# Expert rows added to the output in memory by indirect accumulating writes, in place of stored partial rows and a closing sum

## The chip, the cores and the metric

The kernel runs on one core of a Trainium2 chip. The metric is the device time of one execution in microseconds, as the median of several runs. The engines are called PE (TensorE), DVE (VectorE), ACT (ScalarE), POOL (GpSimd) and SP (SyncE); each runs its own queue of instructions in order and waits on semaphores.

## The reference

A small image tower over 64 images of 2 x 104 x 104: shifted patch tokens, a gated linear attention block, and a mixture of experts with the two best of 8 experts for each token. There are 64 x 170 = 10,880 tokens of 128 numbers. What bears on this case is the last block:

```python
xf = x.reshape(-1, D)                       # layer norm of h, 10880 x 128
logits = xf @ router_w
gate_vals, idx = jax.lax.top_k(logits, 2)
gates = jax.nn.softmax(gate_vals, axis=-1)
out = zeros_like(xf)
for e in range(8):
    h = relu(xf @ w1[e] + b1[e]) @ w2[e] + b2[e]
    y = layernorm(xf + h, gamma[e], beta[e])
    w = sum(where(idx == e, gates, 0.0), axis=-1)
    out = out + w[:, None] * y
result = h + out
```

So each output row is its row of h plus two gated expert rows.

## The kernel before

**Stages.** First the images are made into tokens (to about 240 us), then pairs of images go through attention and routing (32 pairs, to about 690 us), then the experts work on tiles of tokens, then a closing stage sums.

**Pair stage.** For each pair DVE, ACT and PE finish h and the routing. POOL scatters each token's normalised row, with its gate and its id in columns 128 and 129, twice into `x_slots`, a table in memory that is sorted by expert (L552, six scatters a pair). SP stores the pair's rows of h in memory (L408, L410).

**Tile stage.** There are `NTILE` = 92 tiles of 256 slots, every one for one expert. They are the worst case: tiles past the last real one hold padding rows. A helper `tiles` runs the engines' work with lags: in iteration i, SP has loaded tile i into one of six buffers `x_sl` (L429, after `y_ready` of tile i-6), PE transposes tile i and runs the first layer of tile i-1 and the second of i-2, ACT applies relu, DVE adds, normalises, scales and gates (tiles i-1 to i-5). POOL adds a bias to the input of tile i-1 (`with_bias`, L573, read by DVE in iteration i+2) and scatters the finished rows of tile i-5 (`scatter_y`, L579), in this order on its queue. A tile's 256 rows go out in two indirect DMAs of 128 rows of 512 bytes. A token's two experts have ids of their own (2 x token and 2 x token + 1), so all rows of `y_tokens` (21,760) are written once and no scatter has to wait for another. Padding ids lie out of bounds and their rows are dropped. DVE writes a tile's rows into one of two buffers `y_sl` and first waits until the scatters of the tile before last have landed:

```python
need(dve, y_gone[n % 2], 32 * (XBUF // 2 * u + n // 2))
```

**Closing stage.** In the tile stage, after the first six tile loads, SP has loaded all rows of h back from memory, spread as 85 rows to a partition (L435, 5.4 MB). When all scatters have landed, SP loads `y_tokens` in 17 parts of 5 rows and two experts for each partition (L449), DVE adds both to h (L1339, 34 adds), and ACT's queue stores the 17 parts in `out` (L1561).

Of the kernel before, what the change touches and what calls it, by code (L numbers as in the profile page):

```python
# [37 lines left out]
FC = FF // 128  # L38
YBUF = 8
PART_ROWS = NTOK // 128  # L40
SUM_ROWS = 5
NSUM = PART_ROWS // SUM_ROWS
XBUF = 6
# [4 lines left out]
XW = 130  # L48
PAD_ID = 2 * NTOK
LAST_TILE_LAG = 5  # L50
# [20 lines left out]
def const_array():  # L71
    cols, width = const_layout()
    c = np.zeros((128, width), np.float32)

    def put(name):
        a, b = cols[name]
        return c[:, a:b]

    put("ident")[:] = np.eye(128)

    wt = np.array([1 if m in (0, HGRID - 1) else 2 for m in range(HGRID)] * GROUP, np.float32)
    img_h = np.repeat(np.arange(GROUP), HGRID)
    img_m = np.concatenate([np.repeat(np.arange(GROUP), GRID), np.full(HROWS - MROWS, -1)])
    for k, img in enumerate((img_h, img_m)):
        same = (img_h[:, None] == img[None, :]).astype(np.float32)
        put("stat_all")[:HROWS, k * HROWS:(k + 1) * HROWS] = same * (1 + 2 * wt[:, None])
        put("stat_edge")[:HROWS, k * HROWS:(k + 1) * HROWS] = -same * wt[:, None]
    s = np.arange(CHUNK)
    put("causal")[:CHUNK] = s[:, None] <= s[None, :]
    r = np.arange(128)  # L90
    put("before")[:] = r[:, None] < r[None, :]
    put("eo")[:] = (r[:, None] // HK) % 2 == np.arange(2)[None, :]
    h = np.arange(128) // HV
    put("meanv")[:] = (h[:, None] == h[None, :]) / HV
    put("reset")[:] = (np.arange(TOK) % CHUNK != 0)[None, :]
    put("cls_sel")[0, :PT] = np.arange(PT) % TOK != 0
    put("cls_sel")[1, :PT] = np.arange(PT) % TOK == 0
    put("expert")[:] = np.arange(8)
    put("region")[:] = np.arange(8) * REGION
    put("eps")[:, 0:5] = [EPS_TOK, EPS_LN, EPS_GN, EPS_FFN, 1.0]  # L100
    put("eps")[:, 5] = -1 / 16
    put("eps")[:, 6] = 1 / 16
    put("tokid")[:] = 2 * (r[:, None] + 128 * np.arange(PTILES)[None, :])
    put("slotid")[:] = np.arange(128)[:, None] + 128 * np.arange(2)[None, :]
    put("tiles_k")[:] = SLOT * np.arange(43)
    put("one_row")[:] = 1
    return c


def need(eng, sem, value):  # L110

    if not isinstance(value, int) or value > 0:
        eng.wait_ge(sem, value)
# [44 lines left out]
def build(nc, a, out_rows):  # L158

    cols, cwidth = const_layout()  # L160
    xs_dram = nc.dram_tensor("x_slots", (NEXP * REGION + SLOT, XW), F32, kind="Internal").ap()
    h1_dram = nc.dram_tensor("h1_rows", (NTOK, E_DIM), F32, kind="Internal").ap()
    y_dram = nc.dram_tensor("y_tokens", (2 * NTOK, E_DIM), F32, kind="Internal").ap()

    with ExitStack() as ctx:
# [75 lines left out]
        def two(*shape, **kw):  # L241
# [55 lines left out]
        y_id = [A3.take(2, dt=I32) for _ in range(2)]  # L297
        y_tok = [A3.take(SUM_ROWS, 2, E_DIM) for _ in range(YBUF)]
        h1_rows = h[:, :, :, :].rearrange("p a c n -> p (a c n)")[:, 0:PART_ROWS * E_DIM]
        assert A3.at <= PHASE1_WORDS  # L300
# [8 lines left out]
            "c_loaded z_prep w_loaded small_loaded prep_done xl0 xl1 edge_done dsum_done asum_done "  # L309
            "stat_ps var_done h_out h1_stored h1_loaded ln1_stats ln1_rstd xn_ready xnt_ps xnt_sb qk_ps carry_ps g_ps v_ps "  # L310
            "l_ready scan_done e_ready g_copied g_ready v_ready qk_ready sc_ps att_ready kt_ps kt_ready "
# [5 lines left out]
            "xs1 xs2 xs3 xs4 xs5 norm_ready scl_ready gate_ready bns3_ready xt_ps xhi_ready xlo_ready "  # L317
            "h_ps h_ready w2_ps xb_ready t_ready rstd3_stats rstd3_ready y_ready yg0 yg1 yl0 yl1 yl2 yl3 "
            "yl4 yl5 yl6 yl7 sum_ready rstd0_done nb_done xmn_done xhn_done tr_full tr_free y_full "
            "h_added dch ach pch t_prep d_prep xen_done "  # L320
# [9 lines left out]
        TOKEN_BANKS = (4, 5, 7, 4)  # L330
        y_loaded = [S[f"yl{n}"] for n in range(YBUF)]
        LAST_LAG = 5
# [57 lines left out]
        def expert_sync(sp):  # L390
# [14 lines left out]
            with sp.Fori(0, PAIRS) as p:  # L405
                sp.wait_ge(S["h1_ready"], p + 1)
                full = 128 * (PTILES - 1)
                sp.dma_start(h1_dram[bass.ds(p * PT, full), :].rearrange("(c r) n -> r c n", r=128),  # L408
                             h[:, bass.ds(p, 1), 0:PTILES - 1, :].rearrange("p o c n -> p (o c) n")).then_inc(S["h1_stored"], 16)
                sp.dma_start(h1_dram[bass.ds(p * PT + full, PREST), :],  # L410
                             h[0:PREST, bass.ds(p, 1), PTILES - 1, :].rearrange("p o n -> p (o n)")).then_inc(S["h1_stored"], 16)
# [20 lines left out]
            for n in range(XBUF):  # L432
                load(n, n)
            sp.wait_ge(S["h1_stored"], 32 * PAIRS)
            sp.dma_start(h1_rows, h1_dram.rearrange("(p j) n -> p (j n)", p=128)).then_inc(S["h1_loaded"], 16)  # L435
            with sp.Fori(1, NTILE // XBUF) as u:
                for n in range(XBUF):
                    load(XBUF * u + n, n)
            for i in range(NTILE // XBUF * XBUF, NTILE):
                load(i, i % XBUF)  # L440


            for gone in y_gone:
                sp.wait_ge(gone, 32 * (NTILE // 2))

            y_part = y_dram.rearrange("(p j k) n -> p j k n", p=128, k=2)
            for c in range(NSUM):
                need(sp, S["sum_ready"], 2 * (c - YBUF + 1))
                sp.dma_start(y_tok[c % YBUF], y_part[:, SUM_ROWS * c:SUM_ROWS * c + SUM_ROWS]).then_inc(y_loaded[c % YBUF], 16)  # L449

# [61 lines left out]
        def _(pool):  # L512
# [44 lines left out]
            pool.memset(pad_row[:, :, 0:129], 0.0).then_inc(S["pad_ready"], 1)  # L557
            pool.memset(pad_row[:, :, 129:130], float(PAD_ID)).then_inc(S["pad_ready"], 1)

# [15 lines left out]
            def scatter_y(i, n, u, e):  # L575
                pool.wait_ge(S["y_ready"], i + 1)
                apart(pool)
                for k in range(2):
                    pool.indirect_dma_start(  # L579
                        y_dram, bass.IndirectOffsetOnAxis(ap=y_id[n % 2][:, k:k + 1], axis=0),  # L580
                        y_sl[n % 2][:, k, :], None, bounds_check=2 * NTOK - 1, oob_is_err=False,
                    ).then_inc(y_gone[n % 2], 16)

# [3 lines left out]

            pool.wait_ge(S["tab_ready"], 1)
            tiles(pool, Chain(pool, None), 0, 0, tile_iteration)


# [307 lines left out]
        def _(dve):  # L899
# [277 lines left out]
            def gates(p, par):  # L1177
# [4 lines left out]
                ch.step(dve.reciprocal(row[p % ROWS][:, 0, :, 128], den[:, :]))  # L1182
                dve.tensor_scalar(row[p % ROWS][:, 1, :, 129], ids[:, :], 1.0, None, ALU.add).then_inc(S["gate_done"], 1)

            def place(p, par):
# [3 lines left out]
                ch.step(dve.tensor_tensor(row[p % ROWS][:, 1, :, 128], row[p % ROWS][:, 0, :, 128], edif[:, :], ALU.mult))  # L1189
                ch.link(dve.tensor_scalar(ids[:, :], ids[:, :], float(2 * PT), None, ALU.add))  # L1190
                dve.tensor_copy(slot_i[p % ROWS][:], slot_f[:]).then_inc(S["slots_ready"], 1)  # L1191
# [25 lines left out]
            ch.link(dve.memset(om[:, PTILES:PTILES + 1], 0.0))  # L1217
            ch.link(dve.memset(o_f[:, PT:PCOLS], 0.0))
            dve.tensor_copy(ids[:, :], con("tokid")).then_inc(S["base_ready"], 1)  # L1219
            dve.wait_ge(S["base_ready"], 1)  # L1220
# [85 lines left out]
            def shifted(i, n, u, e):  # L1306
# [3 lines left out]

                need(dve, y_gone[n % 2], 32 * (XBUF // 2 * u + n // 2))
                ch.step(dve.tensor_copy(y_id[n % 2], x_sl[n][:, :, E_DIM + 1]))
# [18 lines left out]
            dbase = tiles(dve, ch, dbase, DVE_TILE, tile_iteration)  # L1331


            dve.wait_ge(S["h1_loaded"], 16)
            for c in range(NSUM):
                dve.wait_ge(y_loaded[c % YBUF], 16 * (c // YBUF) + 16)
                rows = h1_rows[:, SUM_ROWS * E_DIM * c:SUM_ROWS * E_DIM * (c + 1)].rearrange("p (j n) -> p j n", n=E_DIM)
                for k in range(2):
                    dve.tensor_tensor(rows, rows, y_tok[c % YBUF][:, :, k, :], ALU.add).then_inc(S["sum_ready"], 1)  # L1339
                    dve.wait_ge(S["sum_ready"], 2 * c + k + 1)  # L1340


        @block.scalar
        def _(act):
# [211 lines left out]

            out_part = out_rows.rearrange("(p j) n -> p (j n)", p=128)
            for c in range(NSUM):
                act.wait_ge(S["sum_ready"], 2 * c + 2)
                part = slice(SUM_ROWS * E_DIM * c, SUM_ROWS * E_DIM * (c + 1))  # L1560
                act.dma_start(out_part[:, part], h1_rows[:, part]).then_inc(S["h_out"], 16)  # L1561
            act.wait_ge(S["h_out"], 16 * NSUM)

# [26 lines left out]
```

## Time and profile before

| what | value |
|---|---|
| median of 3 runs | 1102.32 us (1100.51 to 1102.33) |
| profiled execution, its own time | 1104.65 us |
| span in its profile | 1102.9 us |
| mean granted clock of PE | 0.853 |
| first scatter of tile 0, last scatter of tile 91 (start) | 721.0 us, 1057.1 us |
| last part summed | from 1098.6 us |

Times in the profile count from the start of the span. A row of the timeline gives the start, the duration, engine, line, operation and, in brackets, the idle time of the engine before it with what ended it. "issue" there means that nothing which the profile shows was waited for. The duration of a DMA_INDIRECT on POOL is the time that POOL works on it; its rows land later. In a DMA row each digit is the busy share, in tenths, of the 16 DMA engines in one of 40 equal slices of the window (9 is 90% or more).

### The profile page before, as it was taken

To read this page: it belongs to the slowest core of one execution; us is meant where nothing else is said; L and a number is where in the kernel's file an instruction comes from. 1 tells how busy PE (TensorE), PEld (TensorE's weight loads), DVE (VectorE), ACT (ScalarE), POOL (GpSimd) and SP (SyncE) were. 2 spreads that over 40 slices of the span, in tenths; PEclk is the share of its full clock that TensorE was granted. 3 is DMA by queue.
4 is the path that set the end of the run, shared out by engine and by line. 5 is a ranking of instruction groups with operands and counts; after the bars stand their busy time and mean duration, and the time that the engine had idled before them with its cause. 6 is when DMAs were issued, how large, how long until landed. Compare 5 with 4: busy or idle time off the path is not lost.

```text
span 1102.9 us, 27762 instructions
## 1 busy us (share of the span) xinstructions
PE 880.8 (80%) x7792; PEld 730.5 (66%) x7793; DVE 789.5 (72%) x3172; ACT 554.0 (50%) x1512; POOL 445.1 (40%) x491
## 2 busy tenths in 40 slices
PE   1577888879899999988989973499999999899900
PEld 1467888865676666666667652388888888888800
DVE  1488887754766666667776655189999998899956
ACT  0212111006867666677787642266666666566600
POOL 3000000000144444444554445267777777777720
PEclk9989888898867777789997765699999999999955
DMA  7363441015011111111111111632222222222259
GB/s 132 62 94 51 67 65 23 1 57 165 24 37 43 40 40 40 39 42 50 45 46 47 42 45 40 204 137 75 67 71 70 72 69 66 70 70 73 61 210 397
DMA packets 69073, 84.09 MB, mean 76 GB/s; under 512 B 12051, under 2 KB 53702, under 8 KB 68858
## 3 DMA queue, kind: packets, MB, share of 16 engines
q1 hardware_dynamic: 54282, 54.93, 20.2%
q0 software_dynamic: 12256, 22.50, 6.6%
q10 hardware_dynamic: 2448, 5.57, 1.3%
q8 instruction: 46, 0.75, 0.3%
q14 instruction: 41, 0.34, 0.1%
HBM read 48.15 MB, written 35.71 MB: 76 GB/s over the span
## 4 chain that ended last, share of the span: by engine, by line
PE 52%; issue 14%; DVE 13%; ACT 8%; DMA 5%; another core or an unknown queue 3%; SPq 2%; DVEq 1%; POOL 1%; ACTq 0%; POOLq 0%
PE ps L650 7%; PE ps L885 6%; DVE arena L986 4%; PE ps L706 4%; PE ps L876 4%; PE ps L874 3%; PE ps L731 3%; DMA arena<-y_tokens 3%; PE ps L717 3%; PE ps L875 3%; PE ps L799 2%; PE ps L712 2%; PE ps L766 2%; PE ps L785 2%
## 5 line engine op out<-in xcount | busy, mean ns | idle before, releaser
L552 POOL DMA_INDIRECT x_slots<-arena x192 | 184.2, 959 | 264.2 <-DVE arena L1191 66.5
L579 POOL DMA_INDIRECT y_tokens<-arena x184 | 184.7, 1004 | 46.2 <-issue 43.8
L1538 ACT ACTIVATE arena<-ps,b_t 128x256 f32<-128x256 f32 x368 | 156.8, 478 | 88.3 <-PE ps L876 80.2
L885 PE MATMUL ps<-arena 128*128 x1472 | 181.0, 276 | 0.0
L885 PEld LDWEIGHTS ps<-arena 128*128 128x128 f32 x1472 | 171.6, 192 | 1.9
L650 PE MATMUL ps<-wt,arena 128*128 128x128 f32 x960 | 131.0, 299 | 8.7 <-DVE h L1008 8.7
L650 PEld LDWEIGHTS ps<-wt,arena 128*128 128x128 f32 x960 | 125.6, 213 | 10.2 <-DVE arena L986 10.2
L874 PE MATMUL ps<-arena 128*128 128x256 f16 x368 | 101.5, 276 | 21.2 <-DVE arena L1263 12.4
L1401 ACT ACTIVATE arena<-ps 128x340 f32<-128x340 f32 (+3 forms) x160 | 70.0, 447 | 65.8 <-PE ps L793 24.2
L876 PE MATMUL ps<-arena 128*128 128x256 f16 x368 | 100.9, 274 | 0.0
L875 PE MATMUL ps<-arena 128*128 128x256 f16 x368 | 100.9, 274 | 0.0
L573 POOL TENSOR_TENSOR arena<-arena 128x256 f32<-128x256 f32 x92 | 66.4, 721 | 66.1 <-issue 34.7
L1294 DVE TENSOR_SCALAR arena<-arena 128x128 f32<-128x128 f32 x184 | 88.8, 531 | 3.4
L986 DVE TENSOR_TENSOR arena<-ps,arena 128x312 f32<-128x312 f32 (+2 forms) x160 | 71.1, 502 | 27.2 <-PE ps L636 27.2
L557 POOL MEMSET arena<- 128x258 f32 x1 | 0.3, 318 | 201.4 <-DVE arena L1219 201.4
L1263 DVE TENSOR_TENSOR arena<-ps,arena 128x256 f16<-128x256 f32 x92 | 38.8, 422 | 43.3 <-ACT arena L1530 40.7
L1102 DVE TENSOR_TENSOR arena<-ps,cst 85x340 f32<-85x340 f32 x128 | 59.6, 501 | 13.0 <-PE ps L731 7.7
L874 PEld LDWEIGHTS ps<-arena 128*128 x368 | 35.8, 97 | 39.9 <-issue 34.0
L731 PE MATMUL ps<-arena 32*85 32x170 f32 x512 | 59.2, 353 | 1.6 <-DVE arena L1093 1.6
L1315 DVE SCALAR_TENSOR_TENSOR arena<-arena 128x128 f32<-128x128 f32 x184 | 56.6, 349 | 0.0
L636 PE MATMUL ps<-cst,arena 112*128 112x112 f32 (+1 forms) x216 | 33.2, 286 | 26.6 <-DVE arena L969 26.6
L799 PEld LDWEIGHTS ps<-rw,arena 128*128 128x128 f32 x192 | 35.0, 260 | 28.5 <-ACT arena L1401 16.2
(203 smaller groups left out, 1844.4 us busy)
## 6 DMA issues: line engine op xcount, KB each, us to landing
arena<-x_slots SPq DMA_DIRECT2D x92, 130.0 KB
arena<-y_tokens SPq DMA_DIRECT2D x17, 640.0 KB, 14.8
h<-h_rows SPq DMA_DIRECT2D x1, 5440.0 KB
out<-h ACTq DMA_DIRECT2D x17, 320.0 KB, 9.5
arena<-x_in SPq DMA_DIRECT2D x64, 84.5 KB
arena<-x_in SPq DMA_DIRECT2D x64, 78.0 KB
h_rows<-h SPq DMA_DIRECT2D x32, 128.0 KB
x_slots<-arena POOLq DMA_INDIRECT x192
```

Of the source, the lines that this page charges most:

```text
L552: pool.indirect_dma_start(xs_dram, bass.IndirectOffsetOnAxis(ap=slot_i[n][0:rows, t, k:k + 1], axis=0), row[n][0:rows, k, t, :], None).the ...
L579: pool.indirect_dma_start(y_dram, bass.IndirectOffsetOnAxis(ap=y_id[n % 2][:, k:k + 1], axis=0), y_sl[n % 2][:, k, :], None, bounds_check= ...
L650: ins = pe.matmul(ps[TOKEN_BANKS[pair]][:, 128 * t:128 * t + 128], gx_all[par][:, s, at:at + 128], wt[:, s, :], start=s == 0, stop=s == NS ...
L731: ins = pe.matmul(o, kd[par][r, chunk(c)], qd[par][r, :, chunk(c)], start=True, stop=True, tile_position=(at, 0))
L874: pe.matmul(o, hi, x_hi[m], start=True, stop=False)
L875: pe.matmul(o, hi, x_lo[m], start=False, stop=False)
L876: pe.matmul(o, lo, x_hi[m], start=False, stop=True).then_inc(S["h_ps"], 1)
L885: ins = pe.matmul(ps[6 + m][:, 128 * k:128 * k + 128], hid[m][:, c, 128 * k:128 * k + 128], w2_sb[:, bass.ds(e, 1), c, :].rearrange("p o n ...
L986: return dve.tensor_tensor(dst, src, gm, ALU.mult)
L1294: ins = dve.tensor_scalar(nrm[:, k, :], res[n % 2][:, k, :], mv3[:, k, 0:1], rg3[:, k:k + 1], ALU.subtract, ALU.mult)
L1401: act.activation(dst, src, ACT.Copy).then_inc(S[done], 1)
L1538: act.activation(hid[m][:, c, :], ps[2 + 2 * m + c // 2][:, SLOT * (c % 2):SLOT * (c % 2) + SLOT], ACT.Relu, bias=b1_t[:, bass.ds(e * FC + ...
```

## The change

The rows of h are stored straight into `out`, which has 256 rows more than there are tokens. Both expert rows of a token carry the token's own id, and the scatters add to `out` in memory instead of writing to `y_tokens`. The two experts of a token are in different tiles, so POOL waits, before it scatters a tile, until both scatters of the tile ahead have landed. Padding rows are given ids in the 256 extra rows, which are cleared by two small stores from POOL; no bounds check is left, and padding rows are written too. The load of h, the 17 loads of partial rows, the 34 sums and the 17 stores are dropped, and POOL waits at its end for the last scatters.

```diff
-YBUF = 8
+YBUF = 2
-PAD_ID = 2 * NTOK
+OUT_ROWS = NTOK + SLOT
-    put("tokid")[:] = 2 * (r[:, None] + 128 * np.arange(PTILES)[None, :])
+    put("tokid")[:] = r[:, None] + 128 * np.arange(PTILES)[None, :]
...
-                sp.dma_start(h1_dram[bass.ds(p * PT, full), :].rearrange("(c r) n -> r c n", r=128),
+                sp.dma_start(out_rows[bass.ds(p * PT, full), :].rearrange("(c r) n -> r c n", r=128),
...
-            sp.wait_ge(S["h1_stored"], 32 * PAIRS)
-            sp.dma_start(h1_rows, h1_dram.rearrange("(p j) n -> p (j n)", p=128)).then_inc(S["h1_loaded"], 16)
...
-            for gone in y_gone:
-                sp.wait_ge(gone, 32 * (NTILE // 2))
-            y_part = y_dram.rearrange("(p j k) n -> p j k n", p=128, k=2)
-            for c in range(NSUM):
-                need(sp, S["sum_ready"], 2 * (c - YBUF + 1))
-                sp.dma_start(y_tok[c % YBUF], y_part[:, SUM_ROWS * c:SUM_ROWS * c + SUM_ROWS]).then_inc(y_loaded[c % YBUF], 16)
...
-            pool.memset(pad_row[:, :, 129:130], float(PAD_ID)).then_inc(S["pad_ready"], 1)
+            pool.wait_ge(S["pad_ready"], 2)
+            for m in range(YBUF):
+                pool.dma_start(out_rows[NTOK + 128 * m:NTOK + 128 * m + 128, :], pad_row[:, m, 0:E_DIM]).then_inc(y_gone[m], 16)
...
             def scatter_y(i, n, u, e):
                 pool.wait_ge(S["y_ready"], i + 1)
+                pool.wait_ge(y_gone[(n - 1) % YBUF], 16 + 32 * (XBUF // YBUF * u + (n - 1) // YBUF + 1))
                 apart(pool)
                 for k in range(2):
                     pool.indirect_dma_start(
-                        y_dram, bass.IndirectOffsetOnAxis(ap=y_id[n % 2][:, k:k + 1], axis=0),
-                        y_sl[n % 2][:, k, :], None, bounds_check=2 * NTOK - 1, oob_is_err=False,
-                    ).then_inc(y_gone[n % 2], 16)
+                        out_rows, bass.IndirectOffsetOnAxis(ap=y_id[n % 2][:, k:k + 1], axis=0),
+                        y_sl[n % 2][:, k, :], None, compute_op=ALU.add,
+                    ).then_inc(y_gone[n % YBUF], 16)
...
             pool.wait_ge(S["tab_ready"], 1)
+            pool.wait_ge(S["h1_stored"], 32 * PAIRS)
+            for gone in y_gone:
+                pool.wait_ge(gone, 16)
             tiles(pool, Chain(pool, None), 0, 0, tile_iteration)
+            for gone in y_gone:
+                pool.wait_ge(gone, 16 + 32 * (NTILE // YBUF))
...
-                dve.tensor_scalar(row[p % ROWS][:, 1, :, 129], ids[:, :], 1.0, None, ALU.add).then_inc(S["gate_done"], 1)
+                dve.tensor_copy(row[p % ROWS][:, 1, :, 129], ids[:, :]).then_inc(S["gate_done"], 1)
...
-                need(dve, y_gone[n % 2], 32 * (XBUF // 2 * u + n // 2))
+                dve.wait_ge(y_gone[n % YBUF], 16 + 32 * (XBUF // YBUF * u + n // YBUF))
...
-            dve.wait_ge(S["h1_loaded"], 16)
-            for c in range(NSUM):
-                dve.wait_ge(y_loaded[c % YBUF], 16 * (c // YBUF) + 16)
-                rows = h1_rows[:, SUM_ROWS * E_DIM * c:SUM_ROWS * E_DIM * (c + 1)].rearrange("p (j n) -> p j n", n=E_DIM)
-                for k in range(2):
-                    dve.tensor_tensor(rows, rows, y_tok[c % YBUF][:, :, k, :], ALU.add).then_inc(S["sum_ready"], 1)
-                    dve.wait_ge(S["sum_ready"], 2 * c + k + 1)
...
-            out_part = out_rows.rearrange("(p j) n -> p (j n)", p=128)
-            for c in range(NSUM):
-                act.wait_ge(S["sum_ready"], 2 * c + 2)
-                part = slice(SUM_ROWS * E_DIM * c, SUM_ROWS * E_DIM * (c + 1))
-                act.dma_start(out_part[:, part], h1_rows[:, part]).then_inc(S["h_out"], 16)
-            act.wait_ge(S["h_out"], 16 * NSUM)
```

## Rows read from the trace of the kernel before

**Rows 1.** The page: its span and its 40 slices, tenths of each.

```profile
span 1102.9 us, 27762 instructions
...
PEclk9989888898867777789997765699999999999955
...
DMA  7363441015011111111111111632222222222259
```

**Rows 2.** Windows of 100 us over tiles: engines' busy us and counts, clock, DMA share, GB/s.

```profile
740.00:840.00 100.00, 94.44 (x814) 85.65 (x812) 91.85 (x355) 63.64 (x190) 73.79 (x82) 1.00 0.26 71
...
sum 300.00, PE 281.24 PEld 256.05 DVE 272.94 ACT 191.39 POOL 221.04; mean PE 93.75 PEld 85.35 DVE 90.98 ACT 63.80 POOL 73.68
```

**Rows 3.** Timeline, POOL alone, one tile.

```profile
802.69 0.71 POOL L573 TENSOR_TENSOR arena<-arena 128x256 f32<-128x256 f32 x1 [0.51 <-issue]
...
803.56 1.00 POOL L579 DMA_INDIRECT y_tokens<-arena  x1 [0.15 <-issue]
...
804.86 0.98 POOL L579 DMA_INDIRECT y_tokens<-arena  x1 [0.30 <-issue]
...
806.33 0.72 POOL L573 TENSOR_TENSOR arena<-arena 128x256 f32<-128x256 f32 x1 [0.49 <-issue]
```

**Rows 4.** One line's instructions, L579: ns min/median/max, first and last start.

```profile
L579 POOL DMA_INDIRECT y_tokens<-arena x184: 982/998/1225, 721.0 to 1057.1; - x184
```

**Rows 5.** Timeline, the first tiles.

```profile
701.06 6.13 SPq L429 DMA_DIRECT2D arena<-x_slots  x6
...
703.30 0.29 PEld L859 LDWEIGHTS ps<-cst,arena 128*128 128x128 f32 x2 [14.23 <-DMA arena<-x_slots]
...
707.23 0.47 SPq L435 DMA_DIRECT2D h<-h_rows  x1
...
721.00 1.03 POOL L579 DMA_INDIRECT y_tokens<-arena  x1 [0.16 <-issue]
...
724.59 0.73 POOL L573 TENSOR_TENSOR arena<-arena 128x256 f32<-128x256 f32 x1 [1.15 <-issue]
```

**Rows 6.** Timeline, last scatters and the closing stage.

```profile
1055.86 0.98 POOL L579 DMA_INDIRECT y_tokens<-arena  x1 [0.31 <-issue]
1057.14 0.98 POOL L579 DMA_INDIRECT y_tokens<-arena  x1 [0.30 <-issue]
1059.32 22.52 SPq L449 DMA_DIRECT2D arena<-y_tokens  x17
1063.21 6.83 DVE L1339 TENSOR_TENSOR h<-h,arena 128x640 f32<-128x640 f32 x8 [8.28 <-DMA arena<-y_tokens]
...
1098.58 1.68 DVE L1339 TENSOR_TENSOR h<-h,arena 128x640 f32<-128x640 f32 x2 [0.66 <-DMA arena<-y_tokens]
```

**Rows 7.** Groups by line, closing stage: busy us, mean ns | idle before, releaser.

```profile
L1339 DVE TENSOR_TENSOR h<-h,arena 128x640 f32<-128x640 f32 x34 | 28.0, 825 | 17.3 <-DMA arena<-y_tokens 16.6
```

**Rows 8.** DMA view, 805.84 to 807.20 us, behind a tile's second scatter.

```profile
DMA  0000000000000000399973000000000000000000
...
DMA packets 32, 0.07 MB, mean 48 GB/s; under 512 B 16, under 2 KB 16, under 8 KB 32
```

**Rows 9.** DMA view, 1057.0 to 1059.3 us, last scatters.

```profile
DMA  0000000011000000000000000000001100000000
...
DMA packets 64, 0.00 MB, mean 1 GB/s; under 512 B 64, under 2 KB 64, under 8 KB 64
```

**Rows 10.** DMA view, 701.0 to 703.4 us, the first tile load.

```profile
DMA  0000000000000000003965999886321000000445
```

**Rows 11.** One line's instructions, L552.

```profile
L552 POOL DMA_INDIRECT x_slots<-arena x192: 920/957/1211, 294.0 to 694.0; - x192
```

**Rows 12.** Windows of the pair stage and of the first tiles, columns as in rows 2.

```profile
448.00:452.00 4.00, 2.71 (x22) 1.89 (x21) 2.42 (x15) 2.17 (x7) 1.34 (x2) 1.00 0.12 33
452.00:456.00 4.00, 4.00 (x20) 2.51 (x19) 2.45 (x8) 3.56 (x12) 1.90 (x2) 0.50 0.07 21
...
700.00:710.00 10.00, 4.63 (x24) 3.11 (x25) 0.85 (x2) 2.34 (x6) 1.36 (x2) 0.60 0.54 150
```

More of the change, by code:

```diff
@@ L38 @@
 FC = FF // 128
-YBUF = 8
-PART_ROWS = NTOK // 128
-SUM_ROWS = 5
-NSUM = PART_ROWS // SUM_ROWS
+YBUF = 2
 XBUF = 6
@@ L161, in build @@
     xs_dram = nc.dram_tensor("x_slots", (NEXP * REGION + SLOT, XW), F32, kind="Internal").ap()
-    h1_dram = nc.dram_tensor("h1_rows", (NTOK, E_DIM), F32, kind="Internal").ap()
-    y_dram = nc.dram_tensor("y_tokens", (2 * NTOK, E_DIM), F32, kind="Internal").ap()
     with ExitStack() as ctx:
@@ L297, in build @@
         y_id = [A3.take(2, dt=I32) for _ in range(2)]
-        y_tok = [A3.take(SUM_ROWS, 2, E_DIM) for _ in range(YBUF)]
-        h1_rows = h[:, :, :, :].rearrange("p a c n -> p (a c n)")[:, 0:PART_ROWS * E_DIM]
         assert A3.at <= PHASE1_WORDS
@@ L309, in build @@
             "c_loaded z_prep w_loaded small_loaded prep_done xl0 xl1 edge_done dsum_done asum_done "
-            "stat_ps var_done h_out h1_stored h1_loaded ln1_stats ln1_rstd xn_ready xnt_ps xnt_sb qk_ps carry_ps g_ps v_ps "
+            "stat_ps var_done h1_stored ln1_stats ln1_rstd xn_ready xnt_ps xnt_sb qk_ps carry_ps g_ps v_ps "
             "l_ready scan_done e_ready g_copied g_ready v_ready qk_ready sc_ps att_ready kt_ps kt_ready "
@@ L317, in build @@
             "xs1 xs2 xs3 xs4 xs5 norm_ready scl_ready gate_ready bns3_ready xt_ps xhi_ready xlo_ready "
-            "h_ps h_ready w2_ps xb_ready t_ready rstd3_stats rstd3_ready y_ready yg0 yg1 yl0 yl1 yl2 yl3 "
-            "yl4 yl5 yl6 yl7 sum_ready rstd0_done nb_done xmn_done xhn_done tr_full tr_free y_full "
+            "h_ps h_ready w2_ps xb_ready t_ready rstd3_stats rstd3_ready y_ready yg0 yg1 "
+            "rstd0_done nb_done xmn_done xhn_done tr_full tr_free y_full "
             "h_added dch ach pch t_prep d_prep xen_done "
@@ L330, in build @@
         TOKEN_BANKS = (4, 5, 7, 4)
-        y_loaded = [S[f"yl{n}"] for n in range(YBUF)]
         LAST_LAG = 5
@@ L407, in expert_sync @@
                 full = 128 * (PTILES - 1)
-                sp.dma_start(h1_dram[bass.ds(p * PT, full), :].rearrange("(c r) n -> r c n", r=128),
+                sp.dma_start(out_rows[bass.ds(p * PT, full), :].rearrange("(c r) n -> r c n", r=128),
                              h[:, bass.ds(p, 1), 0:PTILES - 1, :].rearrange("p o c n -> p (o c) n")).then_inc(S["h1_stored"], 16)
-                sp.dma_start(h1_dram[bass.ds(p * PT + full, PREST), :],
+                sp.dma_start(out_rows[bass.ds(p * PT + full, PREST), :],
                              h[0:PREST, bass.ds(p, 1), PTILES - 1, :].rearrange("p o n -> p (o n)")).then_inc(S["h1_stored"], 16)
@@ L1189, in place @@
                 ch.step(dve.tensor_tensor(row[p % ROWS][:, 1, :, 128], row[p % ROWS][:, 0, :, 128], edif[:, :], ALU.mult))
-                ch.link(dve.tensor_scalar(ids[:, :], ids[:, :], float(2 * PT), None, ALU.add))
+                ch.link(dve.tensor_scalar(ids[:, :], ids[:, :], float(PT), None, ALU.add))
                 dve.tensor_copy(slot_i[p % ROWS][:], slot_f[:]).then_inc(S["slots_ready"], 1)
@@ L1218, in _ @@
             ch.link(dve.memset(o_f[:, PT:PCOLS], 0.0))
+            dve.tensor_scalar(pad_row[:, :, 129], con("slotid"), float(NTOK), None, ALU.add).then_inc(S["pad_ready"], 1)
             dve.tensor_copy(ids[:, :], con("tokid")).then_inc(S["base_ready"], 1)
@@ L1587 @@
         aps[name] = nc.dram_tensor(name + "_in", arr.shape, DT.from_np(arr.dtype), kind="ExternalInput").ap()
-    out = nc.dram_tensor("out", (NTOK, E_DIM), F32, kind="ExternalOutput").ap()
+    out = nc.dram_tensor("out", (OUT_ROWS, E_DIM), F32, kind="ExternalOutput").ap()
     build(nc, aps, out)
     r = run_bass_kernel_spmd(nc, [arrays], core_ids=[0])
-    return r.results[0]["out"].reshape(BATCH, TOK, E_DIM)
+    return r.results[0]["out"][:NTOK].reshape(BATCH, TOK, E_DIM)
```

## The prediction

> **What bounds the kernel now.** I read the page first: the last two slices show the DMA engines at five and nine tenths after a long stretch at two, and PE's clock, granted in full through that stretch, at half [rows 1]. Two stages matter, the expert tiles and the closing stage.
>
> The three windows of 100 us over the tile stage show PE busy 94%, DVE 91% and POOL 74% on the mean, with the DMA engines at a quarter [rows 2]. That makes POOL look the least loaded of the three. The timeline of POOL says otherwise [rows 3]: a bias add of 0.72 us, 0.15 us, the first scatter (1.00), 0.30, the second scatter (0.98), and 0.49 until the next bias add: 3.64 us from one bias add to the next. The gaps are put down to "issue", that is to no other engine, and the 0.30 between two scatters stays when nothing else is left to do [rows 6]. So POOL is walked through without a real wait: its queue is as full as PE's. First scatter of tile 0 at 721.00 and first scatter of tile 91 at 1055.86 [rows 4, 6] give the mean period: 334.86 / 91 = 3.68 us.
>
> The closing stage lies bare. The last scatter ends at 1057.14 + 0.98 = 1058.12; SP loads the partial rows from 1059.32, DVE's first sum starts at 1063.21, the last pair of sums at 1098.58, and the span ends at 1102.9 [rows 6]. The sums take 34 x 0.824 = 28.0 us and wait 16.6 us for their loads [rows 7]. From the last scatter's end to the end of the span: 44.8 us.
>
> **What goes.** All of those 44.8 us, except what the last scatter needs to land. The single load of the stored rows into h (SP, 707.23 [rows 5]) goes too. It moves 5.4 MB while tiles 0 to 5 are already in SBUF or on their way; the first reload behind it feeds tile 6, and POOL then shows a gap of 1.15 us [rows 5]. Tile 0's first scatter at 721.00 comes after DVE's first result and not after this load. I cost the removal at nothing if POOL paces the tiles, since an early slip is then absorbed, and at 1 to 2 us gained if it doesn't. The two pad stores that POOL now issues early stand ahead of its first slot scatter at 294.0 [rows 11], whose data the pair stage has yet to make, so they are covered; without that cover they cost two issues of about 1 us. The ids count tokens instead of twice tokens and one add of 1 becomes a copy: one small DVE operation for another, nothing. The wait for the stored rows ahead of the tile loop is nothing too: they stand on SP's queue ahead of the slot loads, and PE waits 14.23 us for the first of those [rows 5].
>
> **What comes in.** Scatter of tile i may not start before both scatters of tile i-1 have landed. Behind that wait on POOL stand its own two scatters and the bias add of tile i+5; that add is used by DVE two tiles later, so DVE follows only when POOL is slower on the whole. DVE's own wait, for the rows of tile i-2, is then always met ahead of time, or one period behind POOL.
>
> The loop on POOL becomes: end of the second scatter, R until the next tile's first scatter may start, first scatter, gap, second scatter. P = R + 1.00 + 0.30 + 1.00 = R + 2.30.
>
> R for plain rows can be read. In the closing case nothing else moves: generation ends at 1058.12 and SP, which waits for this landing, issues at 1059.32: 1.20 us [rows 6]. That scatter moved no rows (0.00 MB in the window), and its small packets pass in slices 31 and 32 of a window of 2.3 us, so until 0.72 us after its end [rows 9]. For a scatter with rows I take the second scatter of a full tile: its generation ends at 805.84 [rows 3], and from there the rows pass in slices 17 to 22 of a window of 1.36 us, that is from 0.54 to 0.75 us after the end, and the small packets behind them [rows 8]. That is about 0.1 us later than the empty one: R = 1.3 us. Today POOL's bias add and its gaps take 0.49 + 0.72 + 0.15 = 1.36 us in the same place [rows 3]. A plain landing would thus be hidden to the last tenth, and P = 3.6, under the 3.68 of today.
>
> But the rows are now added, so each of 128 rows of 512 bytes must be read from HBM before it is written. No row shows this. Lower bound of the extra: 0, if the read is hidden under the descriptor work. Upper bound: a whole further transfer, as the first slot load: issued at 701.06, PE released by it at 703.30, so 2.2 us [rows 5]. Its packets begin only in slice 19 of 40 (2.4 us from 701.00, so at about 702.1) [rows 10]: about 1.0 us of it is the issue, of which the scatter has its own within R, and 1.2 us are the trip with its burst. I take 0.9 us, nearest to that trip, and less than it because the scatter's burst is shorter (0.2 us against some 0.8). R = 1.3 + 0.9 = 2.2 and P = 4.5 us.
>
> Generation: 1.00 us for a scatter with a bounds check, 0.957 us for the one without [rows 4, 11]. The check goes (-0.04), the add may need more descriptor work (unknown; bound above by a half more, 1.5 us, if a row needs a second source beside its source and destination; below by 0.96). I take 1.00.
>
> **Sum.** T = 721.00 + 91 P + 2.30 + R + 0.3 (end of program) = 721.00 + 409.5 + 2.3 + 2.2 + 0.3 = 1135.3 us of span. Against the profiled execution's own span of 1102.9 that is +32.4: the 44.8 us of the closing stage less 2.5 for the last landing are won, 42.3; the tiles cost 91 x (4.50 - 3.68) = 74.6. The profiled execution took 1104.65, the median is 1102.32; moved by the same difference the forecast is 1135 us. The change pays only while 92 R < 1102.9 - 723.6 - 209.3 = 170.0, so R < 1.85 us: half a microsecond beyond a plain landing is what it can bear. Everything hangs on that.
>
> Two rules of the Trainium skill speak against my 0.9. "DMA: Bandwidth & Descriptors", section "Latency and other measured facts", gives 0.2 us for an average HBM access and 2 us at high load. No row here shows an access by itself. As an estimate from that page, with 0.2 us the period would be 3.8 and the span about 1071 us, with 2 us 5.6 and about 1236 us. The same page, section "Two DMAs through the same engine are not ordered", reports that a second read-modify-write of a row read stale data when it directly followed the first and no longer with five packets between. No run here shows this either. By it the write trails the read by some packets only, and a packet run as short as [rows 8] would make the extra a fraction of a microsecond, which is rival A.
>
> **Rivals.**
> A, faster: the read of the old row is hidden. The eight rows of each DMA engine pass in one burst of 0.2 us (16 large packets for 0.07 MB beside 16 small ones, so 4 KB each) [rows 8]; if read and write overlap as closely, R stays between 1.3 and 1.85. At 1.3 the tiles keep 3.68 and T = 721.0 + 334.9 + 2.3 + 1.3 + 0.3 = 1059.8, -43 us, so 1059. It decides from R = 1.85 down. For it speaks the short burst and DMA engines three quarters idle; against it that every row needs two memory trips in order.
> B, generation grows to 1.5 us: P = 2.2 + 3.3 = 5.5, T = 1227. Nothing in the profile prices it.
> C, the read is a full transfer of 2.2 us: R = 3.5, P = 5.8, T = 1255. Beyond it, the eight rows of an engine go one after the other, 8 x 0.9: P = 10.8 and over 1700 us.
> D, PE's clock: with P = 4.5 PE is busy 3.45 us of a tile (93.75% of 3.68 [rows 2]), 77%. The pair stage shows PE busy 2.71 of 4 us at full clock and the next 4 us at half [rows 12]. If the clock is at half for half the time, a tile needs 3.45 / 0.75 = 4.6 us, just above 4.5: T = 1144. Against it, the clock came back in the first 10 us of tiles with PE busy 4.63 of 10 us, and then stayed [rows 1, 12].
>
> **Chances.** Likeliest (extra 0.6 to 1.4 us) 0.50, with its own range 1107 to 1181. A 0.22, of which 0.02 lands within 0.2% of before (2.2 us, about what a measurement of this kernel can tell from no change). B 0.12, C 0.08, its serial form 0.04, D 0.04. Faster 0.20, same 0.02, slower 0.78. The range of 1070 to 1235 leaves out the best part of A (some 0.08) and C with its serial form (0.12).
>
> **What would show it.** In the changed trace POOL's first scatter of a tile should be released by a DMA onto out, not by "issue", and start R after the end of the second scatter: 2.2 us right, below 1.85 and the forecast's sign is wrong. The scatters' own duration tells B. The windows should show PE at about 77% and POOL about 60% at a granted clock of 1.00; lower tells D. Nothing should follow the last scatter but its landing. A second burst or a longer one behind each scatter would show where the read sits.

## The result and the profile after

| what | before | after |
|---|---|---|
| median | 1102.32 us | 1296.92 us (1293.95 to 1305.03, 4 runs) |
| ratio | 1 | 1.178, 95% interval 1.172 to 1.185 |
| profiled execution, its own time and span | 1104.65, 1102.9 us | 1293.95, 1292.1 us |

The sign was right, the size was not: 17.8% slower where 3% was forecast, and 62 us above the upper end of the range. Ratios and ranges, here and below, leave out executions at a lower granted clock that took over 1.5% longer than the fastest of the same kernel, such as one of the kernel before at 1122.55 us.

The page of the changed kernel, its span, clock and DMA slices, POOL's busy slices and its costliest group; beside [rows 1, 4]:

```profile
span 1292.1 us, 27549 instructions
...
POOL 2000000003444444444443466666666666666664
PEclk9988888895886779789655997988898989898985
DMA  7353320411111111111113233323332333333322
...
L563 POOL DMA_INDIRECT out<-arena x184 | 298.7, 1623 | 204.3 <-issue 113.0
...
L556 POOL TENSOR_TENSOR arena<-arena 128x256 f32<-128x256 f32 x92 | 113.9, 1238 | 24.6 <-DVE arena L1260 12.6
```

The scatters are L563 now and the bias adds L556. A scatter takes 1.62 us of POOL on the mean, against 1.00 in [rows 4]. The closing burst of the DMA engines is gone, and the tile stage runs to the end of the span.

POOL alone in the timeline, one tile in the middle and the last two tiles; beside [rows 3, 6]:

```profile
902.31 1.56 POOL L563 DMA_INDIRECT out<-arena  x1 [1.80 <-DMA out<-arena]
904.18 1.56 POOL L563 DMA_INDIRECT out<-arena  x1 [0.30 <-issue]
905.19 1.26 POOL L556 TENSOR_TENSOR arena<-arena 128x256 f32<-128x256 f32 x1
909.01 1.56 POOL L563 DMA_INDIRECT out<-arena  x1 [2.56 <-issue]
...
1277.27 1.56 POOL L563 DMA_INDIRECT out<-arena  x1 [2.43 <-issue]
1279.14 1.56 POOL L563 DMA_INDIRECT out<-arena  x1 [0.30 <-issue]
1283.12 1.56 POOL L563 DMA_INDIRECT out<-arena  x1 [2.42 <-issue]
1284.99 1.56 POOL L563 DMA_INDIRECT out<-arena  x1 [0.30 <-issue]
```

Tile 0's first scatter starts at 721.39, that of tile 91 at 1283.12: P = 561.73 / 91 = 6.17 us, against 3.68 before and 4.50 forecast. Without generation (2 x 1.623) and the gap of 0.30 that leaves R = 2.63 us on the mean; the undisturbed end shows 2.42. The idle time in brackets counts from the bias add where one lies between, and half of it is put down to "issue": the name of the releaser alone would not have told of the wait.

The wait itself is an instruction of POOL's sequencer. The same line's instructions in a small window that holds only the wait ahead of the scatter at 1283.12, columns as in [rows 4]:

```profile
L122 POOLq EVENT_SEMAPHORE  x1: 4852/4852/4852, 1277.5 to 1277.5; - x1
```

It is released at 1277.5 + 4.85 = 1282.4. The scatter ahead of it ended generating at 1280.70, so its rows landed 1.7 us later, and the next scatter starts 0.75 us after the release. R, the time from the end of a tile's second scatter to the start of the next tile's first, is thus made of two parts, 1.7 and 0.75.

The windows over tiles, columns as in [rows 2]:

```profile
740.00:840.00 100.00, 65.27 (x485) 57.30 (x485) 49.51 (x208) 38.71 (x113) 63.57 (x48) 0.90 0.31 43
...
sum 500.00, PE 327.47 PEld 288.20 DVE 248.74 ACT 195.82 POOL 321.35; mean PE 65.49 PEld 57.64 DVE 49.75 ACT 39.16 POOL 64.27
```

PE, DVE and ACT all stand at 39 to 65%: they follow POOL, which is itself busy only 64% and waits in its loop for the rest. DVE's wait ahead of its cast of the ids shows it, in the waits of 740 to 1240 us (engine and line, releaser: us in total, times, longest):

```profile
DVE arena L1302 <- DMA out<-arena: 242.1, 82, 4.6
...
POOL out L563 <- DMA out<-arena: 91.3, 49, 2.1
```

The DMA view behind the second scatter of the tile before the last, 1280.7 to 1283.1 us, beside [rows 8]:

```profile
DMA  0000000009995399999930000000000000000000
...
DMA packets 144, 0.07 MB, mean 27 GB/s; under 512 B 16, under 2 KB 144, under 8 KB 144
```

144 packets where a plain scatter has 32: every added row is a packet of its own (128, and 16 small ones), and they pass in slices 10 to 21 of 0.06 us, so from 0.54 to 1.26 us after the end of generation, where the plain rows were through at 0.75.

The end of the program, by line, last instructions:

```profile
L160 POOLq DRAIN  x1: 3413/3413/3413, 1288.4 to 1288.4; - x1
```

POOL drains for 3.4 us behind its last landing. Before, its drain (8.0 us from 1056.1) lay under the closing stage.

### The profile page after: what moved, and what is told of

The parts are those of the page before. It is cut to its first block and busy times, and to the rows that moved or that the text cites. A ratio compares the mean times of both kernels' runs of the same rounds, so it can differ in the third digit from the quotient of the medians.

```text
span 1292.1 us, 27549 instructions
## 1 busy us (share of the span) xinstructions
PE 933.9 (72%) x7792; PEld 770.2 (60%) x7793; DVE 734.4 (57%) x3139; ACT 557.1 (43%) x1512; POOL 560.0 (43%) x492
## 5 line engine op out<-in xcount | busy, mean ns | idle before, releaser
L563 POOL DMA_INDIRECT out<-arena x184 | 298.7, 1623 | 204.3 <-issue 113.0
L863 PE MATMUL ps<-arena 128*128 128x256 f16 x368 | 113.8, 309 | 182.1 <-DVE arena L1253 182.1
L874 PE MATMUL ps<-arena 128*128 x1472 | 196.9, 291 | 0.0
L874 PEld LDWEIGHTS ps<-arena 128*128 128x128 f32 x1472 | 189.4, 208 | 2.0
L1302 DVE CAST arena<-arena 128x2 int32<-128x2 f32 x92 | 15.5, 169 | 266.3 <-DMA out<-arena 266.3
L863 PEld LDWEIGHTS ps<-arena 128*128 x368 | 39.5, 107 | 206.2 <-issue 197.9
L1526 ACT ACTIVATE arena<-arena,cst 128x2 f32<-128x2 f32 x92 | 27.2, 295 | 275.1 <-DVE arena L1274 269.3
L556 POOL TENSOR_TENSOR arena<-arena 128x256 f32<-128x256 f32 x92 | 113.9, 1238 | 24.6 <-DVE arena L1260 12.6
L865 PE MATMUL ps<-arena 128*128 128x256 f16 x368 | 114.8, 312 | 0.0
L864 PE MATMUL ps<-arena 128*128 128x256 f16 x368 | 114.4, 311 | 0.0
L1284 DVE TENSOR_SCALAR arena<-arena 128x128 f32<-128x128 f32 x184 | 64.0, 463 | 3.4
L706 PE MATMUL ps<-wproj,arena 128*85 128x128 f32 x256 | 46.0, 336 | 14.0 <-ACT arena L1382 14.0
```

The lines of the kernel that those rows point to most:

```text
L556: pool.tensor_tensor(x_b2[n % 2], x_sl[n][:, :, 0:E_DIM], b2, ALU.add).then_inc(S["xb_ready"], 1)
L563: pool.indirect_dma_start(out_rows, bass.IndirectOffsetOnAxis(ap=y_id[n % 2][:, k:k + 1], axis=0), y_sl[n % 2][:, k, :], None, compute_op= ...
L863: pe.matmul(o, hi, x_hi[m], start=True, stop=False)
L864: pe.matmul(o, hi, x_lo[m], start=False, stop=False)
L865: pe.matmul(o, lo, x_hi[m], start=False, stop=True).then_inc(S["h_ps"], 1)
L874: ins = pe.matmul(ps[6 + m][:, 128 * k:128 * k + 128], hid[m][:, c, 128 * k:128 * k + 128], w2_sb[:, bass.ds(e, 1), c, :].rearrange("p o n ...
```

## The experiments

The experiments ran on three chips, on which the kernel before takes different times: 997 us on the chip of the first four, 1094 to 1110 us on the next, and 1069 to 1081 us on that of the last three (half the width and the second and third with float16). So each is compared with the runs of before beside it. On the chip of the first four the stage ahead of the tiles is shorter: the first scatter starts at 640 to 643 us, not at 721. The kernel before wasn't profiled there. Its period is worked out from its time: 997.45 - 1.75 (time less span, as in the profiled execution) - 44.8 (closing stage) - 2.3 (the last tile's two scatters and gap) - 641 = 307.6, by 91, 3.38 us.

**Plain writes, wait kept** (the add is left out, a row of out holds the last expert row):

```diff
-                        y_sl[n % 2][:, k, :], None, compute_op=ALU.add,
+                        y_sl[n % 2][:, k, :], None,
```

> The changed kernel with plain scatters instead of adding ones (the add is left out, so a row of out holds the expert row that came last); every wait stays. Theory 1, the add makes all of the loss: generation back at 0.96 to 1.00 us, R (end of a tile's second scatter to the start of the next tile's first) 1.3 us, period 3.68 us, about 1064 us. Theory 2, the wait has a price of its own, because POOL's sequencer can prepare the next scatter only once it is released: generation 1.00, R 1.2 + 0.75 = 1.95 us, period 4.25 us, about 1115 us. Theory 3, only the wait matters and plain rows land as late as added ones: R 2.4 to 2.6, period 4.8, about 1160 us with generation at 1.00, or 1290 us if the generation of 1.56 us comes from waiting too.

Measured: 1051.08 us against 997.45, ratio 1.052 (1.045 to 1.059). The scatters, then POOL's last tiles, then the wait ahead of the scatter at 1041.42:

```profile
L563 POOL DMA_INDIRECT out<-arena x184: 955/962/1257, 642.5 to 1042.7; - x184
```

```profile
1038.40 0.96 POOL L563 DMA_INDIRECT out<-arena  x1 [0.30 <-issue]
1041.42 0.96 POOL L563 DMA_INDIRECT out<-arena  x1 [2.06 <-issue]
```

```profile
L122 POOLq EVENT_SEMAPHORE  x1: 3257/3257/3257, 1037.4 to 1037.4; - x1
```

Generation is back at 0.96 us. R is 2.06 us: released at 1037.4 + 3.26 = 1040.66, so 1.3 us of landing and 0.76 us from the release to the scatter. The period is (1041.42 - 642.5) / 91 = 4.38 us, where theory 2 said 4.25. That is theory 2: waiting for a plain landing costs R = 2.06 and not 1.3, and 2.1 on the mean of all tiles. The end is dearer than thought: the last scatter's generation ends at 1043.64 and the span at 1051.3, 5.9 us of it POOL's drain.

**The wait alone**, on the kernel before:

```diff
                 pool.wait_ge(S["y_ready"], i + 1)
+                need(pool, y_gone[(n - 1) % 2], 32 * (XBUF // 2 * u + (n - 1) // 2 + 1))
```

> The kernel before with the wait alone: scatter of tile i waits for the landed rows of tile i-1, plain writes to the stored partial rows, closing stage kept. Theory 1 (the add makes the loss): R 1.3 us, period 3.68, 1102 us, no change. Theory 2 (the wait has a price of about 0.75 us in POOL's sequencer): R 1.95, period 4.25, plus 91 x 0.57 = 52 us, 1154 us. Theory 3 (plain rows land as late): R 2.4, period 4.7, 1195 us.

Measured: 1097.95 us, ratio 1.098 (1.090 to 1.106), +100 us. A tile of POOL in its timeline:

```profile
901.40 0.98 POOL L580 DMA_INDIRECT y_tokens<-arena  x1 [0.30 <-issue]
902.38 0.71 POOL L573 TENSOR_TENSOR arena<-arena 128x256 f32<-128x256 f32 x1
904.48 1.00 POOL L580 DMA_INDIRECT y_tokens<-arena  x1 [1.38 <-issue]
```

R = 904.48 - 902.38 = 2.10 here. The period over all tiles is 4.48 us. Against the 3.38 us of before that is 91 x 1.10 = 100 us, but as 3.38 was worked out from the same total, this only says that the start and the closing stage are as assumed; this trace has them, with the first scatter at 643.4 and 44.9 us from the last scatter's end to the end of the span. The expectation had the period nearly right (4.25) and the price wrong, because it took 3.68 for the kernel before. The bias add starts with no gap behind the scatter here, so the gap of 0.49 us ahead of it in [rows 3] was not POOL's own.

The sequencer's own instructions show what lies between the release and the scatter. The wait of this tile, the two moves that belong to the next scatter (902.38 to 904.48 us), and the same two moves of the kernel before, for the scatter at 803.56 of [rows 3]:

```profile
L125 POOLq EVENT_SEMAPHORE  x1: 2977/2977/2977, 900.7 to 900.7; - x1
```

```profile
L580 POOLq MOVE  x2: 29/29/29, 903.7 to 904.3; - x2
```

```profile
L579 POOLq MOVE  x2: 29/29/29, 802.7 to 803.3; - x2
```

The rows have landed at 900.70 + 2.98 = 903.68, 1.3 us after the end of generation. Only then come the moves, and the scatter 0.8 us behind the release. In the kernel before the moves ran at 802.7 and 803.3, under the bias add (802.69 to 803.40), and the scatter followed it after 0.15 us.

**The add alone**, on the kernel before, without the wait. Each stored row is touched once (SP fills them with rows of h in the pair stage, and POOL waits for that fill ahead of the tiles, so the output holds h three times). Of the edit only the scatter is shown:

```diff
-                        y_sl[n % 2][:, k, :], None, bounds_check=2 * NTOK - 1, oob_is_err=False,
+                        y_sl[n % 2][:, k, :], None, bounds_check=2 * NTOK - 1, oob_is_err=False, compute_op=ALU.add,
```

> The kernel before with adding scatters and no wait between tiles: each row of the stored partial rows is still touched once (SP fills them with rows of h in the pair stage first, so the output holds h three times); closing stage kept. Theory 1 and 2 agree that generation grows to 1.56 us a scatter without any wait: POOL's loop is 0.49 + 0.72 + 0.15 + 1.56 + 0.30 + 1.56 = 4.8 us, 1102 + 91 x 1.1 = about 1203 us, or 4.25 us and 1153 us if the bias add overlaps the scatter's end, as it does by 0.55 us in the changed trace. Rival: the longer generation comes from the missing bounds check or from waiting; then 1.00 us and 1102 us here.

Measured: 1091.31 us, ratio 1.092 (1.085 to 1.099), +94 us. By line, then one tile of the timeline:

```profile
L584 POOL DMA_INDIRECT y_tokens<-arena x184: 1562/1567/1809, 640.1 to 1045.3; - x184
```

```profile
805.40 1.57 POOL L584 DMA_INDIRECT y_tokens<-arena  x1 [0.17 <-issue]
807.27 1.56 POOL L584 DMA_INDIRECT y_tokens<-arena  x1 [0.30 <-issue]
808.27 1.27 POOL L578 TENSOR_TENSOR arena<-arena 128x256 f32<-128x256 f32 x1
809.71 1.57 POOL L584 DMA_INDIRECT y_tokens<-arena  x1 [0.16 <-issue]
```

The longer generation belongs to the adding form: it is there with the bounds check and without any wait. POOL is full here, its bias add even starts 0.56 us before the scatter ahead ends, and the next scatter follows 0.88 us behind that end. The period is 4.43 us (4.25 expected for a bias add that overlaps), 1.05 more than the 3.38 worked out for before.

**Half the rows** in each adding scatter (64 of 128; the other half of the expert rows is left out):

```diff
-                        out_rows, bass.IndirectOffsetOnAxis(ap=y_id[n % 2][:, k:k + 1], axis=0),
-                        y_sl[n % 2][:, k, :], None, compute_op=ALU.add,
+                        out_rows, bass.IndirectOffsetOnAxis(ap=y_id[n % 2][0:64, k:k + 1], axis=0),
+                        y_sl[n % 2][0:64, k, :], None, compute_op=ALU.add,
```

> The changed kernel with 64 rows in each adding scatter instead of 128 (the other half of the expert rows is left out). If descriptor generation goes by the row: 0.8 us a scatter, landing a little earlier, period about 4.4 us, about 1135 us. If it is a fixed cost of the adding form: 1.5 us a scatter, only the burst of packets is shorter (by half of 0.7 us), period 5.7 to 5.8 us, about 1250 us.

Measured: one run, 1162.1 us on the chip where before takes 997.45.

```profile
L563 POOL DMA_INDIRECT out<-arena x184: 1417/1419/1628, 640.8 to 1151.4; - x184
```

Half the rows take 1.42 of 1.57 us: generation is nearly all fixed. The period is 5.59 us (5.7 to 5.8 expected) and R 2.43 us on the mean. The total was missed (1250 expected) mostly by the start, 80 us earlier on this chip.

**Both kernels again**, on another chip:

> The kernel before, unchanged, for its profile on the chip of these runs. On the chip of the first four experiments it took 997 us, and the first scatters there started at 640 to 643 us instead of 721. If the pair stage alone is shorter, the period is still 3.68 us. From 997.45 less 1.75, less the 44.8 us of the closing stage, less 641 and 2.3: 308.6 / 91 = 3.39 us, so PE and not POOL's queue paces the tiles of the kernel before, and POOL's own shortest loop lies below 3.4 us.

> The changed kernel, unchanged, beside the kernel before on the chip of these runs. If POOL alone paces its tiles, the period stays 6.15 to 6.2 us, though PE is faster here: 641 + 91 x 6.17 + 3.4 + 5.5 + 1.8 = about 1213 us against 997, so +215 us. If the loss were tied to PE's clock, it would stay +194 us or shrink in proportion, 1175 to 1191 us.

The kernel before took 1102.62 us with its first scatter at 719.3 and the period 3.69 us, so on this chip it is the kernel of [rows 1 to 7] again; the first four experiments' chip wasn't met a second time, and its period for before stays worked out, not seen (307.6 us by 91; the 308.6 above is a slip). The changed kernel took 1296.27 us, ratio 1.175 (1.159 to 1.191), with a period of 6.16 us. The question asked of it, whether its loss is the same where the kernel before is faster, stays open for the whole kernel.

**The wait ahead of the bias add**, plain writes (the add is left out; `landed` holds the wait that stood in `scatter_y`):

```diff
             def tile_iteration(at):
+                at(5, landed)
                 at(1, with_bias)
                 at(5, scatter_y)
```

> The first experiment (plain writes, wait kept, add left out) with the wait for the landed rows moved ahead of the bias add on POOL. There the scatter started 0.76 us after the release of the wait. If these 0.76 us are POOL's sequencer preparing the scatter, it does so while the bias add runs: R = 1.31 + 0.1 + 0.7 + 0.15 = 2.25 to 2.35 us, period 4.5 to 4.6. If they are a delay of the release itself, they stand ahead of the bias add too: R = 1.31 + 0.76 + 0.7 + 0.15 = 2.9 us, period 5.15 us.

Measured: one run, 1178.54 us, period 4.89 us, R 2.6 on the mean, between the two forecasts. The timeline says why:

```profile
900.11 0.96 POOL L562 DMA_INDIRECT out<-arena  x1 [0.30 <-issue]
902.87 0.78 POOL L556 TENSOR_TENSOR arena<-arena 128x256 f32<-128x256 f32 x1 [1.80 <-DMA out<-arena]
903.81 0.98 POOL L562 DMA_INDIRECT out<-arena  x1 [0.16 <-issue]
```

The scatter now follows 0.16 us behind the bias add, so its preparation did run under it. But the bias add has a preparation too. The wait's instruction on POOL's sequencer ends at 902.39, 1.3 us behind 901.07, and the bias add starts 0.5 us after it, not 0.1; in between the sequencer works through its registers and one more wait. What stands first behind a wait pays for its own sequencer work, 0.5 us for this bias add, 0.76 for a scatter.

**Half the width** (adding scatters of 64 numbers a row; the other half of each row is left out and the rows land elsewhere in out):

```diff
-                        out_rows, bass.IndirectOffsetOnAxis(ap=y_id[n % 2][:, k:k + 1], axis=0),
-                        y_sl[n % 2][:, k, :], None, compute_op=ALU.add,
+                        out_rows.rearrange("r (a b) -> (r a) b", a=2), bass.IndirectOffsetOnAxis(ap=y_id[n % 2][:, k:k + 1], axis=0),
+                        y_sl[n % 2][:, k, 0:64], None, compute_op=ALU.add,
```

> The changed kernel with adding scatters of 64 numbers (256 bytes) a row instead of 128 numbers, 128 rows each; the other half of each expert row is left out and the rows land elsewhere in out. If the longer generation (1.57 us) is a cost of the adding form and not of bytes, it stays 1.5 to 1.6 us here. If the later landing comes from the bytes that each row reads and writes, the landing is 0.2 to 0.4 us earlier and R 2.2 to 2.4; if it comes from the trip of each row to memory and back, R stays 2.6. Period 5.8 to 6.2 us either way; by rival, a generation that goes by bytes, 0.8 us and period 4.6.

Measured: one run, 1262.4 us.

```profile
L563 POOL DMA_INDIRECT out<-arena x184: 1562/1565/1775, 705.1 to 1253.5; - x184
```

Generation doesn't know the width. The period is 6.01 us, 0.16 less than with the full width, of which R takes it all (2.46 on the mean against 2.63). In the drained end R is 2.43 ahead of the last tile, against 2.42. So half the bytes take off at most a third of the 0.5 us by which added rows land later on the mean, and nothing where no other work is left; whether the rest is the read of the old row or the passing of single packets, no run separates.

**A smaller closing stage instead.** If the closing stage can't be traded for adds, it can be made shorter: the kernel before with its partial rows in float16.

```diff
-    y_dram = nc.dram_tensor("y_tokens", (2 * NTOK, E_DIM), F32, kind="Internal").ap()
+    y_dram = nc.dram_tensor("y_tokens", (2 * NTOK, E_DIM), F16, kind="Internal").ap()
...
-        y_sl = [A3.take(2, E_DIM) for _ in range(2)]
+        y_sl = [A3.take(2, E_DIM, dt=F16) for _ in range(2)]
...
-        y_tok = [A3.take(SUM_ROWS, 2, E_DIM) for _ in range(YBUF)]
+        y_tok = [A3.take(SUM_ROWS, 2, E_DIM, dt=F16) for _ in range(YBUF)]
```

> The kernel before with its stored partial rows in float16 instead of float32 (y_tokens, y_sl, y_tok). No wait, no add in memory. The closing stage moves 5.6 + 5.6 MB instead of 11.1 + 5.6 MB. If it is bound by the DMA engines: 44.8 x 11.2 / 16.7 = 30 us, so 14 us faster than before. If DVE's 34 sums of 0.82 us (28.0 us) or the latency at both ends bound it: 35 to 45 us, 0 to 10 us faster.

The groups by line of its closing stage (beside [rows 7]):

```profile
L1339 DVE TENSOR_TENSOR h<-h,arena 128x640 f32<-128x640 f32 x34 | 28.0, 824 | 8.6 <-DMA arena<-y_tokens 7.5
```

From the last scatter's end to the end of the span it took 36.1 us against 44.6 in the profile of before beside it. DVE is idle 8.6 us instead of 17, of which 7.5 are ahead of its first sum, and then sums in one piece: the DMA engines no longer bind. The whole time doesn't show it: ratio 1.000 (0.988 to 1.011). It was measured again, once as it stands and once with four of the 17 parts summed by POOL, with these lines in the same edit:

```diff
+POOL_PARTS = (3, 7, 11, 14)
...
+            for c in POOL_PARTS:
+                pool.wait_ge(y_loaded[c % YBUF], 16 * (c // YBUF) + 16)
...
+                    pool.tensor_tensor(rows, rows, y_tok[c % YBUF][:, :, k, :], ALU.add).then_inc(S["pool_sum"], 1)
```

> The kernel before with float16 partial rows, once more, for a verdict on time with more rounds. Its closing stage took 36.1 us against 44.6 (from the end of the last scatter's generation to the end of the span), now bound by DVE's 34 sums in a row. 8.5 us of 1100 us, ratio 0.992; by the rival that the difference in the closing stage is lost elsewhere, ratio 1.00.

> As the run beside it, with four of the 17 parts summed by POOL instead of DVE. DVE: 26 sums of 0.824 = 21.4 us instead of 28.0; POOL: 8 sums of 640 numbers, about 1.8 us each by its bias add (0.72 us for 256), 14.4 us beside it. Then the DMA engines (16.7 MB less 5.6) bound the closing stage at about 30 us: 5 us less than the run beside it, ratio to before 0.987. By the rival that the DMA engines already bound at 34 us or that the late POOL parts end last: no further gain.

Float16 alone: ratio 0.999 (0.991 to 1.007), where 0.992 was expected. With POOL's sums: 0.994 (0.990 to 0.999), where 0.987 was expected. But in its profile the closing stage took 38.1 us from 1042.41 to 1080.5, 2 us more than with float16 alone on the same chip (35.9), so the sums on POOL (3.3 to 4.0 us for a part, where DVE takes 1.7) don't explain the gain. That either version beats the kernel before isn't settled; if so, it is by half a percent.

## Why the forecast was too low

Against the sum of the prediction, 1135.3 us of span, the profile shows 1292.1, so 156.8 us more. By its own terms:

| term | forecast | measured | us |
|---|---|---|---|
| first scatter of tile 0 | 721.00 | 721.39 | +0.4 |
| generation, two scatters, 91 tiles | 2.00 | 3.25 | +113 |
| R, 91 times | 2.2 | 2.63 | +39 |
| last tile's own generation | 2.3 | 3.4 | +1 |
| last landing and end of program | 2.5 | 5.55 | +3 |

**The step that failed is "Generation ... I take 1.00".** It was mis-sized: 1.62 us on the mean, just above the upper bound named there (1.5), and it is paid twice a tile on the engine that paces. Rival B had the mechanism and carried 0.12. The add alone shows it without any wait, the plain writes take it away, half the rows and half the width leave it nearly whole. The bound was a guess without a row; with no row for an operation that runs 184 times on the pacing engine, the middle of its bounds would have been the honest value (about 1.25: 45 us more).

**R came out near, by two errors that cancel in part.** Its plain part was read from SP, which issued 1.20 us after the last generation [rows 6]. POOL needs 1.3 us of landing plus 0.76 until its scatter starts: R for plain rows is 2.06. SP's next instruction was a direct DMA of its own; POOL's is an indirect scatter, and behind a wait its sequencer doesn't prepare it ahead, as it does in [rows 3] under the bias add. The part for the add was taken at 0.9; measured are 1.7 against 1.3 in the drained ends of the two profiles, so 0.4, and 2.63 against 2.1 on the mean, so 0.5. Here the page that the prediction weighed, "DMA: Bandwidth & Descriptors" of the Trainium skill, section "Latency and other measured facts", with 0.2 us for an average HBM access, was nearer than the row of a whole load. No run shows an access by itself, nor what else the row's 1.2 us held.

**"POOL's queue is as full as PE's" was wrong**, and with it "a plain landing would be hidden to the last tenth". The trace of the kernel before shows it itself, at a place that the prediction didn't read:

```profile
934.83 1.00 POOL L579 DMA_INDIRECT y_tokens<-arena  x1 [0.16 <-issue]
936.13 0.98 POOL L579 DMA_INDIRECT y_tokens<-arena  x1 [0.30 <-issue]
937.10 0.73 POOL L573 TENSOR_TENSOR arena<-arena 128x256 f32<-128x256 f32 x1
938.00 1.00 POOL L579 DMA_INDIRECT y_tokens<-arena  x1 [0.17 <-issue]
```

Here the bias add starts at the very end of the scatter (0.98 us from 936.13), and POOL's plain loop takes 938.00 - 934.83 = 3.17 us, half a microsecond less than the mean of 3.68. So the gap of 0.49 us under "issue" in [rows 3] was for the most part a wait that had no releaser's name, and a plain landing of 1.3 us couldn't hide in it: what is left between the scatters of two tiles is 0.9 us. The wait alone, without any add, costs 100 us on the chip where 3.38 us a tile were worked out for the kernel before.

The statement that the change pays only for R below 1.85 us stands for the generation that it assumed; with the measured 1.62 us the bound is 0.6 us. And since a plain landing already needs 2.06, no adding scatter however fast could have paid with this wait in this place: plain writes with the wait and no closing stage are 5.2% slower than before on their chip. On the chip of the result, an estimate from the rows is 721.4 + 91 x 4.38 + 2.2 + 7.7 = 1129.9 us of span, 2.4% above 1102.9.

**What was right:** the closing stage goes in full, less the end; the tiles are paced by POOL's loop of two generations, a gap and R, and 721.39 + 91 x 6.17 + 3.4 + 5.5 gives the span; tile 0 starts as before (what the load of h cost the tiles behind it can't be seen under POOL's longer loop); the small edits of the ids and the pad rows show nowhere. Rival A is out with R at 2.63, and rival C (R = 3.5) on the other side. C's serial form is out too: the 128 packets pass in under 0.8 us. Rival D happened a little, the granted clock is 0.90 in the tile windows, and costs nothing, since PE is busy 65% and waits.

The parts don't add up to the whole, and needn't. Against the 3.38 worked out, the wait alone adds 1.10 us and the add alone 1.05; together the loop, measured on other chips at 6.16 and 6.17, is 2.8 longer. Of the missing 0.65 us some 0.5 is the later landing of added rows, which costs time only where something waits for it, and 0.2 is POOL's waiting time in the kernel before (3.38 - 3.17), out of which each pays a part when it is alone. What does add up is POOL's loop: 3.17 plain, 1.3 more with the wait (4.48 measured), 1.25 more with the longer generation (4.43 measured), and with both and the 0.5 for the landing 6.2.

## What to carry to other kernels

Before a wait on landed rows is put ahead of a scatter on POOL, price the loop as landing + the sequencer's own time behind a wait + all generations, here 1.3 + 0.76 + 2.2 = 4.3 us with plain rows (measured 4.38), and take the time behind the wait from the engine that will wait, not from another. An adding scatter of 128 rows costs POOL 1.56 to 1.78 us instead of 0.96 to 1.00. Most of it doesn't shrink with the rows or their width (1.42 us with 64 rows), so splitting one costs; more than 128 rows wasn't tried. A gap under "issue" is not proof that an engine is full: look for the shortest such gap in the trace, here 0.0 us against the usual 0.49.

## What wasn't expected of the hardware

- Generation of an adding indirect scatter is 1.57 us for 128 rows of 512 bytes, 1.57 for 256 bytes, 1.42 for 64 rows; plain 0.96 us without and 1.00 with a bounds check.
- An added row is a packet of its own: 144 packets a scatter instead of 32.
- The bias add on POOL starts 0.55 us before an adding scatter ends, and then shows 1.26 us instead of 0.72; behind plain scatters it doesn't. Spans on POOL are rough, so whether it runs or is only issued then stays open.
- POOL's drain at the end took 3.4 us with adds and 5.9 us with plain writes, where it isn't hidden, and 8.0 us in the kernel before, where it is. What makes the difference wasn't tried.
